# The lead-in of a macaron block on one NeuronCore: weight maxima spread without diagonals, the gate's scale first, the first block normed by VectorE

## The reference

```
x = x + 0.5 * ffn(layernorm(x))
x = x + linear_attention(layernorm(x)) @ Wo.T + bo
x = x + 0.5 * ffn(layernorm(x))        # same weights

layernorm(x) = (x - mean) / sqrt(var + 1e-5)
ffn(x) = sum over 8 experts of (silu(x @ Wg[e]) * (x @ Wu[e])) @ Wd[e]     # 128 -> 512 -> 128
```

## Time and profile before

| | |
|---|---|
| median of 3 runs | 2052.86 us |
| the profiled execution, first to last instruction | 2050.8 us |
| TensorE busy | 2044.4 us |
| VectorE busy | 1659.4 us |
| ScalarE busy | 1441.0 us |
| GpSimd busy | 707.6 us |

### The profile page before, as it was taken

The page is one execution under the profiler, slowest core; times in us unless marked ns, Lnnn a source line. Parts: engine busy times, 40 slices in busy tenths (PEclk is TensorE's granted clock), DMA queues, the critical chain, the costliest instruction groups (busy, mean ns, idle before and its releaser), DMA issues.

```text
span 2050.8 us, 29511 instructions
## 1 busy us (share of the span) xinstructions
PE 2044.4 (100%) x9495; PEld 931.6 (45%) x9495; DVE 1659.4 (81%) x2747; ACT 1441.0 (70%) x2509; POOL 707.6 (35%) x717
## 2 busy tenths in 40 slices
PE   9999999999999999999999999999999999999999
PEld 5444444444444444444444444444444444444444
DVE  7886787878787878787878787878787878877676
ACT  7777767767776676677766776776677766666665
POOL 6631134334423432335234323523344243431000
PEclk9999999999999999999999999999999999999999
DMA  7031246244633542556245334544355346522100
GB/s 216 16 50 18 69 103 139 52 102 88 136 87 81 106 89 73 92 104 130 58 88 111 73 97 82 104 94 98 68 110 124 93 73 130 113 37 42 21 11 16
DMA packets 248907, 173.88 MB, mean 85 GB/s; under 512 B 162736, under 2 KB 219056, under 8 KB 248752
## 3 DMA queue, kind: packets, MB, share of 16 engines
q1 hardware_dynamic: 213760, 129.27, 26.8%
q0 software_dynamic: 34992, 42.74, 13.1%
HBM read 99.62 MB, written 30.67 MB: 64 GB/s over the span
## 4 chain that ended last, share of the span: by engine, by line
PE 97%; DVE 1%; DMA 1%; POOL 0%; ACT 0%; issue 0%; SPq 0%; DVEq 0%; ACTq 0%; POOLq 0%
PE bank L683 11%; PE bank L680 11%; PE bank L679 11%; PE bank L643 11%; PE bank L644 11%; PE bank L662 11%; PE bank L666 11%; PE bank L650 11%; PE bank L663 11%; PE bank L688 1%; PE bank L687 1%; PE bank L689 1%; DMA turn_scratch<-turn_sb 0%; DMA arena<-in_L_ffn_Wu 0%; DVE h_lo L979 0%
## 5 line engine op out<-in xcount | busy, mean ns | idle before, releaser
L775 ACT ACTIVATE silu_sb<-bank,scal 128x512 f32<-128x512 f32 x1024 | 704.6, 688 | 572.7 <-PE bank L650 562.3
L972 DVE SCALAR_TENSOR_TENSOR bank<-silu_sb,scal,bank 128x512 f32<-128x512 f32 x976 | 731.7, 750 | 365.1 <-ACT silu_sb L775 360.1
L979 DVE TENSOR_TENSOR h_lo<-bank,h_hi 128x512 f16<-128x512 f32 x976 | 667.7, 684 | 0.1
L782 ACT ACTIVATE h_hi<-bank 128x512 f16<-128x512 f32 x976 | 577.4, 592 | 4.0 <-DVE bank L972 3.3
L643 PE MATMUL bank<-xn,wg_hi 128*128 128x512 f16 x1024 | 388.1, 379 | 0.7 <-ACT wg_hi L765 0.7
L662 PE MATMUL bank<-xn,wu_hi 128*128 128x512 f16 x1024 | 388.2, 379 | 0.3 <-DVE h_lo L979 0.2
L666 PE MATMUL bank<-xn,wu_lo 128*128 128x512 f16 x1024 | 388.1, 379 | 0.3 <-POOL wu_lo L1148 0.3
L683 PE MATMUL bank<-h_hi,wd_lo 128*128 128x512 f16 x1024 | 388.1, 379 | 0.0
L663 PE MATMUL bank<-xn,wu_hi 128*128 128x512 f16 x1024 | 388.1, 379 | 0.0
L679 PE MATMUL bank<-h_hi,wd_hi 128*128 128x512 f16 x1024 | 388.1, 379 | 0.0
L680 PE MATMUL bank<-h_lo,wd_hi 128*128 128x512 f16 x1024 | 388.1, 379 | 0.0
(11 more groups left out here) (122 smaller groups left out, 1390.6 us busy)
## 6 DMA issues: line engine op xcount, KB each, us to landing
arena<-rep_scratch SPq DMA_DIRECT2D x128, 512.0 KB, 6.9
arena<-arena POOLq DMA_DIRECT2D x56, 512.0 KB, 4.9
turn_scratch<-turn_sb SPq DMA_DIRECT2D x204, 64.0 KB, 1.9
x_tok<-turn_scratch POOLq DMA_DIRECT2D x51, 256.0 KB, 4.7
rep_scratch<-arena SPq DMA_DIRECT2D x16, 512.0 KB, 2.7
x_tok<-in_L_attn_x SPq DMA_DIRECT2D x16, 256.0 KB, 5.3
term_scratch<-arena SPq DMA_DIRECT2D x8, 512.0 KB, 3.4
arena<-term_scratch SPq DMA_DIRECT2D x8, 512.0 KB, 3.8
```

What stands on the lines that cost most here:

```text
L775: act.activation(silu_sb[:, n % 3, :], gate_ps[n % NG][:, :], ACT.Silu, scale=unscale[G[group(n)]]).then_inc(sem("silu"), 1)
L972: dve.scalar_tensor_tensor(up_ps[n % NUP][:, :] if n >= NF else h_sb(n), silu_sb[:, n % 3, :], (h_scale if n >= N_ALL else h_first)[group(n)],
L979: dve.tensor_tensor(h_lo[:, n % NH, :], up_ps[n % NUP][:, :], h_hi[:, n % NH, :], ALU.subtract).then_inc(sem("h_lo"), 1)
```

## The change

Spreading the maxima: the diagonal matrices are gone. The weight that TensorE loads is now the column of maxima itself, read with step 0 as 128 columns and as the top half of its float32 (`top_half`), and what streams is an identity in bfloat16 (`ident_half`), 128 columns for each maximum. The exponent is masked after the maximum over partitions, one more instruction in `take_scale`.

Gate first: scale 0 is for the first gate weights alone, scale 1 for up. ScalarE makes the first gate weight's high half in two pieces of 256 columns. `gates_first` does the three gate matmuls with the high half of x, then the second spread, then the three with its low half. GpSimd makes the first gate weights' low halves, from a scaled copy by ScalarE; VectorE made the first of these before.

The first block's norm is made by VectorE (`norm_tile`) in four tiles, each of which TensorE may turn at once; ScalarE did it before, from a bias (`shift`) that GpSimd computed. The second block's statistics and norm move from the lead-in to units 3 and 4 of VectorE, its transposes from unit 1 to unit 5 and from `down_ps` to `misc_ps`. Its load is issued behind that of the first down weights, and both behind a wait for block 0's arrival. The numbers of idle matmuls go from 22, 4, 9 to 13, 2, 3.

```diff
-    WARM = (22, 4, 9)
-    SPREADS = [(1, 1), (10, 2), (25, 3)]
+    WARM = (13, 2, 3)
+    SPREADS = [(1, "spread", 2), (5, "norm_T", 1), (10, "spread", 3), (25, "spread", 4)]
...
+    MAXIMA = [(-1, "w_max", (2, 0)), (1, "w_scale", 2), (3, "stats", 1), (3, "aggr", 1), (4, "norm_second", 1),
...
+    pool_at[3].append(("rstd_second", 1))
+    act_at[6].append(("xn_hi", 1))
...
             for w in range(2):
                 load_w(w, 0)
+            sp.wait_ge(sem("x_in0"), 16)
+            load_w(2, 0)
             load_x(1)
-            load_w(2, 0)
...
+            def norm_T_second():
+                pe.wait_ge(sem("norm_second"), 1)
+                take_turn("norm_T", 1)
+                for t in range(TT):
+                    made = pe.transpose(misc_ps[:, cols(t, P)], xn_tok[:, 0, cols(t, P)], ident[:, :])
+                made.then_inc(sem("norm_T"), 1)
...
+            def gates_first():
+                for n in range(NG):
+                    if n == 0:
+                        pe.wait_ge(sem("xn_hi"), 1)
+                        pe.wait_ge(sem("wg_first"), 1)
+                    elif n == NG - 1:
+                        pe.wait_ge(sem("wg_hi"), 1)
+                    pe.matmul(gate_ps[n][:, :], wg_hi[:, cols(n, P)], xn_hi[:, 0, :], start=True, stop=False)
+                spread(1)
+                pe.wait_ge(sem("lo_first"), 1)
+                for n in range(NG):
+                    pe.matmul(gate_ps[n][:, :], wg_hi[:, cols(n, P)], xn_lo[:, 0, :], start=False, stop=False)
...
-            for w in range(2):
-                piece_max(w, 0, amax_row[w])
-            dve.wait_ge(sem("pool_const"), 1)
-            diagonal(0)
-            dve.wait_ge(sem("x_in1"), 16)
-            norm_stats(1, 1, "stats")
-            norm_aggr(1, "stats", 2, "mean_var")
+            dve.wait_ge(sem("mean_var"), 1)
+            dve.tensor_scalar(var_eps[:, 0, :], mean_var[:, 0, :, 1], LN_EPS, None, ALU.add).then_inc(sem("var_first"), 1)
+            piece_max(0, 0, amax_row[G[0]])
+            dve.wait_ge(sem("rstd_first"), 1)
+            for t in range(TT):
+                norm_tile(0, 0, t).then_inc(sem("norm_first"), 1)
+            weight_scale(0)
+            piece_max(1, 0, amax_row[U[0]])
             dve.wait_ge(sem("xn_hi"), 1)
             dve.tensor_tensor(xn_lo[:, 0, :], down_ps[:, :], xn_hi[:, 0, :], ALU.subtract).then_inc(sem("lo_first"), 1)
-            weight_scale(0)
+            weight_scale(1)
             group_scales(0)
-            weight_low("g", wg_hi, wg_lo, raw_g, G, 0)
             weight_low("u", wu_hi, wu_lo, raw_u, U, 0)
-            piece_max(2, 0, amax_row[DN[0]])
...
+                    elif kind == "norm_second":
+                        dve.wait_ge(sem("rstd_second"), 1)
+                        dve.wait_ge(sem("norm_T"), 1)
+                        for t in range(TT):
+                            made = norm_tile(1, 1, t)
+                        made.then_inc(sem("norm_second"), 1)
```

More of the change, by code:

```diff
@@ L191, in macaron_program @@
         load[t] += SPARE
-    for t, i in SPREADS:
-        held[t - 1] = held[t] = ("spread", i)
-        pe_at[t].append(("spread", i))
+    for t, kind, i in SPREADS:
+        held[t - 1] = held[t] = (kind, i)
+        pe_at[t].append((kind, i))
+    pool_at[3].append(("rstd_second", 1))
+    act_at[6].append(("xn_hi", 1))
     def blocks_of(b):
@@ L476, in by_vector @@
         def by_vector(w, x):
[L477 removed]
+            return (w, x) == ("u", 0) or (w, x) in VECTOR_LOW
         def low_of(w, x):
@@ L614, in spread, with norm_T_first @@
             def spread(i):
-                pe.wait_ge(sem("w_diag"), i + 1)
-                take_turn("spread", i)
[L617 to L627, removed]
+                k, m = SPREAD[i]
+                if i == 4:
+                    pe.wait_ge(sem("w_row"), 1)
+                else:
+                    pe.wait_ge(sem("w_max"), (1, 2, 3, 6)[i])
+                take_turn("spread", i)
+                for j in range(m):
+                    made = pe.matmul(misc_ps[:, cols(j, P)], top_half(k + j), ident_half[:, :], start=True, stop=True)
+                made.then_inc(sem("spread"), 1)
+            def norm_T_first():
                 for t in range(TT):
+                    pe.wait_ge(sem("norm_first"), t + 1)
                     made = pe.transpose(down_ps[:, cols(t, P)], xn_tok[:, 0, cols(t, P)], ident[:, :])
                 made.then_inc(sem("norm_T"), 1)
+            def norm_T_second():
[16 more added lines that the diff above has]
+                    pe.matmul(gate_ps[n][:, :], wg_hi[:, cols(n, P)], xn_lo[:, 0, :], start=False, stop=False)
             def gate_high(n):
@@ L698, in _ @@
             pe.wait_ge(sem("pool_const"), 1)
-            pe.wait_ge(sem("pool_ones"), 1)
-            norm_T(0)
+            spread(0)
             idle(WARM[1])
-            spread(0)
+            norm_T_first()
             idle(WARM[2])
-            for n in range(NG):
-                gate_high(n)
+            gates_first()
             for n in range(NG):
@@ L749, in _ @@
                     elif kind == "watt_spread":
-                        pe.wait_ge(sem("watt_diag"), 2)
+                        pe.wait_ge(sem("watt_row"), 4)
                         take_turn(kind, i)
-                        pe.matmul(misc_ps[:, :], ones_half[:, :], max_diag.rearrange("p m q -> p (m q)"),
-                                  start=True, stop=True).then_inc(sem("watt_spread"), 1)
+                        for j in range(4):
+                            made = pe.matmul(misc_ps[:, cols(j, P)], top_half(Q + j), ident_half[:, :], start=True, stop=True)
+                        made.then_inc(sem("watt_spread"), 1)
         @block.scalar
@@ L797, in _ @@
             act.activation(warm[:, :], minus_half[:, :], ACT.Silu)
-            act.wait_ge(sem("shift"), 1)
-            for t in range(TT):
-                norm(0, t, 0, "norm")
             act.wait_ge(sem("norm_T"), 1)
             act.activation(xn_hi[:, 0, :], down_ps[:, :], ACT.Copy).then_inc(sem("xn_hi"), 1)
-            weight_high("g", wg_hi, raw_g, G, 0)
+            act.wait_ge(sem("w_scale"), 1)
+            for half in range(2):
+                j = cols(half, FF // 2)
+                act.activation(wg_hi[:, j], raw_g[:, j], ACT.Copy, scale=scale[G[0]]).then_inc(sem(("wg_first", "wg_hi")[half]), 1)
+            act.wait_ge(sem("wg_hi"), 1)
+            scaled("g", raw_g, G, 0)
+            high_half("g", wg_hi, raw_g, G, 1)
             weight_high("u", wu_hi, raw_u, U, 0)
+            act.wait_ge(sem("wg_hi"), 2)
+            scaled("g", raw_g, G, 1)
             for n in range(FIRST, LAST):
```

140 lines of the change are left out of this document (63 added, 77 removed).

## The result

The changed kernel takes 2056.47 us (median of 16 runs, 2055.72 to 2057.56), the kernel before 2052.88 (16 runs beside it, 2052.02 to 2053.28). The ratio is 1.0018, its 95% interval 1.0012 to 1.0025: some 3.6 us slower, which is clear of the noise (the interval lies above 1), but inside the 0.2% that the prediction takes as no change, inside its range, and 1.4 us above its forecast of 2055.1. One execution of the whole study, 2136.52 us in e9_best at a granted clock of 0.949, is of the slow state and is left out of that version's ratio; all others are of the fast one.

The account below looks back on a forecast made before the run. TensorE's lead-in plus a stream without holes bounds the kernel. Unit 6 comes 2.1 us later through the second norm, +2.2 in all: span 2050.8 to 2053.0, plus 2.06 gives 2055.1 us; range 2050.8 to 2058.6, its own 2053.1 to 2056.0.

Parts of the forecast that it names:

- The first gate matmul: Lead-in: the first real matmul on TensorE starts at 9.2 us instead of 13.18, 4.0 us earlier.
- What TensorE finds behind it: From the first gate matmul to the first down's end: small waits, end at 19.0 us, 3.8 us ahead.
- The two small waits: TensorE in the lead-in: about 0.4 us for the low half of x, 0.6 for the gate's low half.
- The second norm: Block 1's transposes wait 5.3 us for VectorE's norm (root done at 22.0); unit 6 at 24.9, +2.1 us.
- Two terms of that chain: VectorE's queue before the second norm: 1.14 us for up's low half (expert 1), 0.77 for the down weights'.
- The tiles: Second block's four norm tiles on VectorE beside GpSimd's low halves of h: 2.4 us, ending at 24.4.
- The clock: TensorE behind its 5.3 us wait: the forecast counted no clock fall; the rival that counts one had chance 0.28.
- the clock rival: Clock falls in TensorE's 5.3 us wait, in some executions only; at worst +2.4 us, 2057.5 us; chance 0.28.
- Behind it: After unit 6: a 0.1 us wait before unit 8, then a full stream; 0.7 us either way for shifts.
- Load order: Loads of block 1 and the down weights come 1 to 2 us later; taken to cost nothing.
- Around the span: From span to median time: 2.06 us added to the forecast span of 2053.0 us.
- The rival "not waited for": VectorE and GpSimd reach the second norm in time, so the lead stays: 2049.6 us; chance 0.10.

Follow-up runs that it names:

- e9_best: Changed kernel with second block's sums early, root and tiles on GpSimd behind its first low half of h, transposes behind unit 6: 2051.93 us, ratio 0.9996.
- e2_hold: Changed kernel, but GpSimd waits for VectorE's four tiles of the second block before its overdue low halves of h: 2054.37 us, ratio 1.0007.
- e7_warm_hold: Changed kernel with GpSimd waiting for the second block's tiles, plus 15 idle matmuls in TensorE's wait for them: 2053.34 us, ratio 1.0001.
- e10_stats: Changed kernel with second block's sums back in VectorE's lead-in and root early on GpSimd; tiles stay on VectorE, behind h of unit 3: 2052.54 us.
- e3_load: Changed kernel with the old load order: second block ahead of the down weights, no wait for the first block's arrival: 2056.4 us, ratio 1.0017.
- e6_late: Changed kernel with the second block's transposes, and its high and low half, behind unit 7 instead of unit 5: 2057.54 us, ratio 1.0022.
- e11_stats_hold: Changed kernel with second block's sums and root early, GpSimd waiting for VectorE's four tiles before unit 2's low half of h: 2050.85 us, ratio 0.999.
- e5_order: Changed kernel with second block's sums in the lead-in, its root, then the first low half of h, then its tiles on GpSimd: 2051.05 us, ratio 0.9992.
- e4_back: Changed kernel with second block's sums in VectorE's lead-in, its root and tiles on GpSimd ahead of the first low half: 2051.39 us, ratio 0.9991.

## Why the prediction was right, and where its sizes were off

**The first gate matmul: right.** Forecast 9.2 with weights at 5.48; measured 10.07 with weights at 6.27, that is 3.80 behind the maximum's start, against 3.72 in the forecast.

**What TensorE finds behind it: right.** The first down's last matmul was put near 19.0 at its end; it starts at 19.59, so its end is near 19.8, or 19.0 for weights at 5.48. The two small waits were put at 0.4 (low half of x) and 0.6 (low half of the gate). By the distance of starts they are 0.3 (L653 starts at 11.06, TensorE was free at some 10.8) and 0.66 (L671 starts at 12.37, free at 11.71). The second agrees by luck: the forecast's own times, 11.3 for that low half and 10.95 for TensorE, give 0.35. Nothing hangs on it, since the next thing, up's low half at 12.6, is set by VectorE: measured 13.38, that is 12.6 for weights at 5.48.

**The second norm: right in place and cause, too small in two terms.** The chain root at 22.0 was 22.49, with weights 0.79 later, so 0.3 sooner than forecast. Two terms of that chain are exchanged: up's low half for expert 1 took 0.74 and not 1.14, that of the down weights 1.09 and not 0.77; their sum hides it. The tiles took 2.80, not 2.4. The forecast scaled three tiles in 1.84; the rule of the Trainium skill that it weighed beside it ("SBUF — State Buffer", section "SBUF: two separate sides", one engine holds the port pair and the other is fully blocked) gave 2.6 to 2.8. The trace agrees with it: two tiles of 1.18 and 1.19, each as long as one low half of 1.16, and two of 0.33. So does e2_hold: the tiles lose 1.7 us and GpSimd next to nothing (2.27 for two, as when the tiles were out of its way). From the tiles' end to unit 6 it was 0.96, not 0.5, as the transposes ran at the slow clock. Sum at unit 6: 2.13 forecast, + 0.79 late weights (chance) - 0.3 + 0.4 + 0.46 = 3.5, as measured.

**The clock: the step that went the other way.** The forecast took no fall and gave the rival 0.28, at 2057.5 us; the fall came in every one of the 16 runs. So the likeliest single case was not what happened: the clock rival's mechanism was, at a smaller price, and 2056.47 lies outside the forecast's own range (to 2056.0) though inside the whole one. The step that failed in the forecast is that it took nothing for the clock behind a wait of 5.3 us because no row of before showed a fall; the longest wait in those rows was 0.7 us, so they could not show one. And two things were wrong in the rival. The price: 2.4 us, half of the 4.9 of the start. In the profile the stream lost 1.3 us (six starts 0.43 apart and one 0.27, instead of 0.216) and the transposes about 0.4: from 22.1 to 25.38 the clock was slow with nothing to run, and that part is free. By medians, e7_warm_hold against e2_hold, it is 1.0; between the runs of e10_stats with and without the fall it is 1.8. So it is 1 to 2 us, and these runs don't say where between. And "in some executions only": with waits of 5.4 us (changed kernel, e3_load), 5.0 (e6_late) and 3.7 (e2_hold) all 49 runs show it, with 2.1 us (e10_stats) 5 of 11. The Trainium skill ("TensorE: Matmul & The Clock Gate", section "HAM oscillation — how this bites in real kernels") says that a long enough idle stretch makes the restart cold; these runs agree.

**Behind it: right.** The stream has no new hole behind unit 8, apart from the slow matmuls. The three small ones of the profile before (0.15, 0.26 and 0.38 us at 135, 929 and 1485 us) are missing after; such holes come and go in all profiles of this study, and when unit 6 came sooner, part of the gain was often given back at 118 to 138 us (0.7 us in e2_hold). Sum from unit 6 to the end: +1.29 - 0.79 = +0.5, measured 2024.93 against 2024.40 us up to the last transposes. **Load order: right**, as far as e3_load can show.

**Around the span: misread.** The forecast added 2.06 us to a span; every run has 1.7 to 1.9 around its span (this one 1.77), and the rest was the distance of one execution from the median. That made the forecast 0.3 too high. In all: 2052.86 + 3.51 + 0.53 + 0.06 (behind the last transposes) - 0.29 = 2056.67, the profiled execution's time. Of the 1.6 us by which this is above 2055.1, the clock is 1.7, and the rest cancels: late weights +0.8, the three holes gone -0.8, root and tiles +0.1, the misread 0.3. That they cancel is luck.

**The rival "not waited for"** would have been 2049.6; e11_stats_hold, which removes most of the wait, measures 2050.85 and keeps 0.9 us of it. So the first part of the change is worth about 2 us, with the second norm's sums in the lead-in; the late second norm, the clock's fall included, takes 5.6. The first is e11 against before; the second e11 against the changed kernel.

## What to carry to other kernels

When an edit starts the busiest engine earlier, follow the other engines' queues to their next hand-over: here the sooner start was real and the norm moved into VectorE's units took it back. A wait that is new and of several us on TensorE is to be charged for its restart as well, 1 to 2 us here. Hold a GpSimd operation that is not yet needed when short VectorE tiles are on the path: one added wait gave 2.1 us in e2_hold and 1.7 in e11_stats_hold, there in part because the clock no longer fell.

## What the runs showed of the hardware

- Four 128x128 scalings on VectorE: 1.11 us alone (e2_hold, e11_stats_hold), 2.80 beside two GpSimd subtractions that start with them, 2.31 when they start in the middle of one and a second follows (e10_stats). A tile that begins just behind a subtraction of GpSimd ends about 0.1 us after it (1.18 and 1.19 us beside 1.16), one without takes 0.33 to 0.35. The same four on GpSimd took 3.55 to 3.62 (e9_best, e5_order, e4_back).
- A single wait in the lead-in costs TensorE its clock: in all 49 runs with waits of 3.7 to 5.4 us, in 5 of 11 with 2.1 us (e10_stats). With idle matmuls in the same wait the mean granted clock stays 1.0 (11 of 11 runs in e7_warm_hold, none of 11 in e2_hold).
- The same first load of 512 KB arrives up to 1.3 us later in one profile than in another (6.27 us against 4.93 or before), and what hangs on it moves with it: unit 6 comes 20.01 us behind it in both the changed kernel and e3_load, at 26.28 and 25.38.
- One edit of the lead-in made one transposing DMA at 1658 us land 14.3 us after its issue, in both profiles of it, with 3.1 us as the median of such DMAs and 11.4 as the slowest in any other version. The cause is open.
